# Batch 3's mixing behind steps with a product, partly on GpSimd, and two context moves later

## The reference, cut to what matters

```python
# first layer, on x of 4 batches x 1024 rows x 128 columns
x = layernorm_g_b(layernorm(x))
last_x = x shifted down by one row
k, v, r = [(x * m + last_x * (1 - m)) @ W.T for m, W in ((mix_k, Wk), (mix_v, Wv), (mix_r, Wr))]
den[t] = den[t-1] * td + exp(k[t]);  num[t] = num[t-1] * td + exp(k[t]) * v[t]     # td = exp(time_decay)
x2 = x0 + (sigmoid(r) * num / (den + 1e-8)) @ Wo.T
# second layer, on layernorm(x2): six nodes, each an attention of 8 heads
for c in range(6):
    q = ew[c,0] * (nodes[c-1] @ We[eq] + be[eq])
    k, v likewise from up to five nodes back
    o = softmax(qh @ kh.T / 4) @ vh, heads joined, @ Wo[c]
    nodes[c] = act_w[c] * o + q
out = x2 + layernorm(nodes[5]) * g + b
```

## Time and profile before

| | |
|---|---|
| median of 3 runs | 2249.14 us (2245.19 to 2252.85) |
| the profiled execution's own time | 2245.28 us |
| span of the profile | 2243.5 us |
| TensorE busy | 2182.0 us, 97% |
| VectorE busy | 2064.3 us, 92% |
| ScalarE busy | 1796.7 us, 80% |
| GpSimd busy | 530.1 us, 24% |
| mean granted TensorE clock | 0.994 |

### The profile page before, as it was taken

How to read it: one execution, slowest core, us unless ns; L and a number is a source line. 1 busy time by engine, 2 the same in 40 slices (tenths; PEclk the granted TensorE clock), 3 DMA queues, 4 the chain that set the end, 5 groups by cost and what they waited for, 6 DMA issues and landing times.

```text
span 2243.5 us, 43662 instructions
## 1 busy us (share of the span) xinstructions
PE 2182.0 (97%) x16565; PEld 885.5 (39%) x16565; DVE 2064.3 (92%) x3252; ACT 1796.7 (80%) x3432; POOL 530.1 (24%) x667
## 2 busy tenths in 40 slices
PE   7999999999999999999999999999999999999997
PEld 3533333343333443443433433433433434434332
DVE  6999999999989999999999999999999999999895
ACT  4377887888778888888888888888888888788776
POOL 4431221312203113123023022022121121431213
PEclk9999999999999999999999999999999999999999
DMA  4230422414223134133232242242242242241301
GB/s 127 65 75 22 83 55 67 81 45 85 60 59 80 50 72 82 53 81 73 54 79 65 58 83 58 56 93 55 59 84 55 57 85 54 59 99 43 75 25 53
DMA packets 87536, 149.39 MB, mean 67 GB/s; under 512 B 35146, under 2 KB 49950, under 8 KB 87326
## 3 DMA queue, kind: packets, MB, share of 16 engines
q0 software_dynamic: 28224, 94.13, 20.0%
q1 hardware_dynamic: 59102, 52.46, 9.4%
HBM read 42.36 MB, written 14.91 MB: 26 GB/s over the span
## 4 chain that ended last, share of the span: by engine, by line
PE 76%; DVE 11%; SPq 7%; DMA 4%; issue 2%; ACT 1%; POOL 0%; POOLq 0%; DVEq 0%; ACTq 0%
PE context L660 28%; PE ring L615 26%; PE wide L639 8%; DVE max_neg L1279 4%; SPq L1593 4%; DVE max_neg L1276 3%; PE wide L550 2%; PE wide L530 2%; PE wide L522 2%; DMA q_aug<-rows_dram 2%; DMA rows_dram<-max_turn 2%; PE wide L555 2%; SPq L1590 1%; PE wide L541 1%; PE context L485 1%
## 5 line engine op out<-in xcount | busy, mean ns | idle before, releaser
L906 ACT ACTIVATE e_ring<-ring 128x512 f32<-128x512 f32 x3053 | 1603.7, 602 | 302.6 <-PE ring L615 300.5
L1276 DVE TENSOR_REDUCE max_neg<-wide 128x1 f32<-128x512 f32 x1800 | 1132.7, 682 | 87.6 <-PE wide L639 84.5
L639 PE MATMUL wide<-k_aug,q_aug 48*128 48x512 f32 x3072 | 1057.3, 440 | 14.0 <-DVE max_neg L1279 6.7
L615 PE MATMUL ring<-q_aug,k_aug 50*128 50x512 f32 x3053 | 1042.6, 437 | 16.1 <-DMA q_aug<-rows_dram 15.2
L660 PE MATMUL context<-e_ring,v_aug 128*32 128x256 f32 (+1 forms) x9240 | 905.0, 463 | 1.0 <-ACT raw L915 0.9
L1279 DVE TENSOR_REDUCE max_neg<-wide 128x2 f32<-128x1024 f32 x636 | 771.8, 1218 | 26.3 <-PE wide L639 20.2
L615 PEld LDWEIGHTS ring<-q_aug,k_aug 50*128 50x128 f32 x3053 | 492.7, 185 | 726.0 <-ACT e_ring L906 608.5
L639 PEld LDWEIGHTS wide<-k_aug,q_aug 48*128 48x128 f32 x3072 | 500.2, 185 | 40.2 <-DVE max_neg L1279 15.8
L660 PEld LDWEIGHTS context<-e_ring,v_aug 128*32 128x32 f32 x9240 | 184.7, 108 | 412.1 <-issue 293.3
L395 POOL DMA_DIRECT2D src<-node_dram x40 | 22.9, 572 | 672.8 <-DMA rows_dram<-max_turn 672.8
L1381 POOL CAST q_part<-q_part 128x512 fp32r<-128x512 f32 x46 | 28.1, 611 | 397.5 <-DVE max_turn L1298 214.2
(11 more groups left out here) (245 smaller groups left out, 938.7 us busy)
## 6 DMA issues: line engine op xcount, KB each, us to landing
q_aug<-q_part POOLq DMA_DIRECT2D x138, 256.0 KB, 4.3
k_aug<-k_part POOLq DMA_DIRECT2D x138, 256.0 KB, 6.5
src<-node_dram POOLq DMA_DIRECT2D x40, 512.0 KB, 7.2
ctxT<-raw SPq DMA_DIRECT2D x380, 32.0 KB, 2.0
rden_bc<-rden_dram SPq DMA_DIRECT2D x23, 512.0 KB
node_dram<-node_ring SPq DMA_DIRECT2D x16, 512.0 KB, 2.7
q_aug<-rows_dram SPq DMA_DIRECT2D x192, 8.0 KB
node_ring<-in_L_attn_x SPq DMA_DIRECT2D x4, 512.0 KB, 5.3
```

Of the source, the lines that this page charges most:

```text
L615: e.matmul(bk[:, :], k_aug[first:first + AUG, u % 2, h // 2, chunk * P:(chunk + 1) * P].bitcast(F32R), q_aug[first:first + AUG, u % 2, h / ...
L639: e.matmul(bk[:, :], q_aug[first:first + SPLIT, u % 2, head // 2, q0:q0 + P].bitcast(F32R), k_aug[first:first + SPLIT, u % 2, head // 2, h ...
L906: e.activation(e_ring[:, n % E_SLOTS, :], bank[where["st", n]][:, :], ACT.Exp, scale=EXP_SCALE).then_inc(a_exp, 1)
L1276: e.tensor_reduce(max_neg[:, G % 2, kh, row:row + 1], wide[:, b, :], AX_X, ALU.max, negate=True).then_inc(v_mx, 1)
```

## The change

It has five parts.

1. **Row mixing on GpSimd.** For i = 6 and 7 the subtraction and the three blends leave VectorE (4 instructions a half) for GpSimd (7 a half: the subtraction, then a multiplication and an addition for each blend).
2. **Denominator product on GpSimd.** PRODUCT for i = 4 to 7 leaves VectorE (1 instruction a half) for GpSimd (2 a half). i = 4 and 5 are in unit 0 and start their product one step earlier.
3. **Batch 3's steps.** All of batch 3's stages now stand at the end of whole steps, and TensorE's stages of it on odd ones. Its TensorE products go to wide banks, behind the attention's product of that step and before the half weighted sum (`late_mix_at`). The table that predicts wide banks counts them.
4. **Two context moves.** The moves of a unit's first two groups, at steps 15 and 17 before, both stand at step 21, behind the rows' store of step 20 and their load. In the last unit this holds for the first group only.
5. **The last outputs.** Of unit 22's output projection, made in unit 23, the first half moves from step 13 to step 15.

A semaphore `v_num` takes the place of an engine-wide count for the numerator scan.

```diff
...
@@ -223,11 +223,13 @@
         LERPED = (6, 7)
+        ON_RING = (TURN, PROJ_K, PROJ_V, PROJ_R, OUT, TURN2)
+        GPSIMD_PRODUCT = (4, 5, 6, 7)
         COLUMNS_AT = 2
         EDGE_TURNS = -(-3 * NODES // 4)
 
         K_AT, OUT_AT, TURN_AT, V_AT, Q_AT = (7, 11), (15, 19), 21, (23, 27), (31, UC + 3)
-        FIRST_K_AT, FIRST_V_AT, FIRST_Q_AT, LAST_OUT_AT, LAST_TURN_AT = (5, 9), (21, 25), (2, 3), (13, 17), 19
+        FIRST_K_AT, FIRST_V_AT, FIRST_Q_AT, LAST_OUT_AT, LAST_TURN_AT = (5, 9), (21, 25), (2, 3), (15, 17), 19
...
-            (U1 + 4.5, U1 + 12.5, U1 + 13, U1 + 18, U1 + 29.5, U2 + 4.5, U2 + 6, U2 + 12.5, U2 + 6, U2 + 10, U2 + 14, U2 + 14,
-             U2 + 16.5, U2 + 29.5, U3 + 4.5, U3 + 12.5, U3 + 12.5, U3 + 16.5, U3 + 19, U3 + 22, U3 + 29.5, U4 + 4.5, U4 + 6, U4 + 10),
...
+            (U1 + 15, U1 + 31, U2 + 1, U2 + 5, U2 + 16, U2 + 16, U2 + 16, U2 + 16, U2 + 21, U2 + 25, U2 + 29, U2 + 29, U2 + 31, U3,
+             U3 + 15, U3 + 15, U3 + 31, U3 + 31, U4, U4 + 5, U4 + 15, U4 + 17, U4 + 18, U4 + 21),
...
-        LATE_R1_AT = {U2 + 22: 6, U5 + 22: 7}
+        LATE_R1_AT = {U2 + 30: 6, U5 + 15: 7}
...
-                taken += len(products(s))
+                taken += len(products(s)) + sum(k in ON_RING for _, k in mix_stages(s))
...
-                        e.wait_ge(v_lerp, 4 * LERPED.index(i) + n + 2)
+                        e.wait_ge(g_lerp, 3 * LERPED.index(i) + n + 1)
...
                 for i, k in mix_stages(s):
                     mix(i, k, next_bank)
 
+            def late_mix_at(s):
+
+                for i, k in mix_stages(s):
+                    mix(i, k, next_max_bank)
...
                 pair(s, 3)
                 pair(s + 1, 0)
                 weighted(s - 1, whole, True, True)
-                mix_at(s)
                 pair(s + 1, 1)
                 pair(s + 1, 2)
                 pair(s + 1, 3)
                 for kind, unit, hf in products(s + 1):
                     product(kind, unit, hf, next_max_bank())
+                late_mix_at(s + 1)
                 weighted(s, first_half, True, False)
-                mix_at(s + 1)
 
             alone[0] = True
             for s in range(ALONE, LAST_STEP):
...
-                if k == LERP_D and i in LERPED:
-                    e.wait_ge(a_xT, i + 1)
-                    e.tensor_tensor(y, xT[:, 1:BANK + 1], xT[:, 0:BANK], ALU.subtract).then_inc(v_lerp, 1)
-                if LERP_K <= k <= LERP_R and i in LERPED:
-                    n = k - LERP_K
-                    e.wait_ge(v_lerp, 4 * LERPED.index(i) + 1)
-                    e.scalar_tensor_tensor(out=(ek, ekv, er)[n], in0=y, scalar=col[:, C_MIX + n:C_MIX + n + 1], in1=xT[:, 0:BANK],
-                                           op0=ALU.mult, op1=ALU.add).then_inc(v_lerp, 1)
...
+                    if i in LERPED:
+                        e.wait_ge(g_lerp, 3 * LERPED.index(i) + 3)
...
-                if k == PRODUCT:
+                if k == PRODUCT and i not in GPSIMD_PRODUCT:
...
+                xT = mixing_xTs[i]
+                if k == LERP_D and i in LERPED:
+                    e.wait_ge(a_xT, i + 1)
+                    e.wait_ge(v_pad, i + 1)
+                    e.wait_ge(p_mt, i + 1)
+                    after()
+                    step(e.tensor_tensor(y, xT[:, 1:BANK + 1], xT[:, 0:BANK], ALU.subtract))
+                if LERP_K <= k <= LERP_R and i in LERPED:
+                    n = k - LERP_K
+                    dst = (ek, ekv, er)[n]
+                    after()
+                    step(e.tensor_scalar(dst, y, col[:, C_MIX + n:C_MIX + n + 1], None, ALU.mult))
+                    after()
+                    signal(e.tensor_tensor(dst, dst, xT[:, 0:BANK], ALU.add), g_lerp)
+                if k == PRODUCT and i in GPSIMD_PRODUCT:
+                    e.wait_ge(v_den, i + 1)
+                    e.wait_ge(v_ekv, i + 1)
+                    after()
+                    step(e.tensor_scalar(ek, y, WKV_EPS, None, ALU.add))
+                    after()
+                    signal(e.tensor_tensor(er, er, ek, ALU.mult), g_prod)
...
-                    if s % NCH == 1 and 0 <= G < GROUPS and G % GPU and G != GROUPS - 3:
+                    if s % NCH == 1 and 0 <= G < GROUPS and G % GPU > 1:
                         move_ctx(G)
                     if s == ALONE + 2:
                         move_ctx(GROUPS - 3)
-                    G = (s - 15) // NCH
-                    if s % NCH == 7 and 0 <= G < GROUPS and G % GPU == 0:
+                    G = (s - 21) // NCH
+                    if s % NCH == 5 and 0 <= G < GROUPS and G % GPU == 0:
                         move_ctx(G)
+                        if G + 1 != GROUPS - 3:
+                            move_ctx(G + 1)
```

More of the change, by code:

```diff
@@ L153, in build @@
         a_exp, a_k1, a_q1, a_oa, a_cv, a_ft, a_high, a_order = sems("a_exp a_k1 a_q1 a_oa a_cv a_ft a_high a_order")
-        v_own, v_omm, v_lerp, v_split0, v_var, v_y, v_pad, v_ekv, v_den, v_prod, v_inv, v_gate, v_x2, v_var2, v_n2 = sems(
-            "v_own v_omm v_lerp v_split0 v_var v_y v_pad v_ekv v_den v_prod v_inv v_gate v_x2 v_var2 v_n2")
+        v_own, v_omm, v_num, v_split0, v_var, v_y, v_pad, v_ekv, v_den, v_prod, v_inv, v_gate, v_x2, v_var2, v_n2 = sems(
+            "v_own v_omm v_num v_split0 v_var v_y v_pad v_ekv v_den v_prod v_inv v_gate v_x2 v_var2 v_n2")
         v_mx, v_cmb, v_neg, v_v, v_rec, v_fvar, v_ctx, v_lvar, v_z = sems(
             "v_mx v_cmb v_neg v_v v_rec v_fvar v_ctx v_lvar v_z")
-        g_own, g_half, g_ident, g_vones, g_kones, g_rs1, g_rs2, g_rsf, g_rsl, g_r1, g_gate = sems(
-            "g_own g_half g_ident g_vones g_kones g_rs1 g_rs2 g_rsf g_rsl g_r1 g_gate")
+        g_own, g_half, g_ident, g_vones, g_kones, g_rs1, g_rs2, g_rsf, g_rsl, g_r1, g_gate, g_lerp, g_prod = sems(
+            "g_own g_half g_ident g_vones g_kones g_rs1 g_rs2 g_rsf g_rsl g_r1 g_gate g_lerp g_prod")
         g_k, g_q, g_norm, g_out, g_y, g_n2, g_fn = sems("g_k g_q g_norm g_out g_y g_n2 g_fn")
@@ L253, in build @@
                              (-12, -12, -11, -10, -9, -9, -7, -6, -5, -5, -1)),
[2 rows of a table removed]
[L256 to L261 removed]
[2 rows of a table added]
+            (U1 + 15, U1 + 31, U2 + 1, U2 + 5, U2 + 16, U2 + 16, U2 + 16, U2 + 16, U2 + 21, U2 + 25, U2 + 29, U2 + 29, U2 + 31, U3,
+             U3 + 15, U3 + 15, U3 + 31, U3 + 31, U4, U4 + 5, U4 + 15, U4 + 17, U4 + 18, U4 + 21),
+            (U2 + 5, U2 + 21, U4 + 23, U4 + 29, U5, U5, U5, U5, U5 + 5, U5 + 9, U5 + 13, U5 + 13, U5 + 15, U5 + 16,
+             U5 + 31, U5 + 31, U6 + 1, U6 + 7, U6 + 9, U6 + 13, U6 + 15, U6 + 17, U6 + 18, U6 + 21))
+        LATE_R1_AT = {U2 + 30: 6, U5 + 15: 7}
         VALUES_FREE_AT = 18
@@ L1074, in mix @@
                     done = e.tensor_tensor_scan(num, td, ekv, 0.0 if hf == 0 else keep[1], ALU.mult, ALU.add)
-                    step(done)
+                    done.then_inc(v_num, 1)
                     if hf == 0:
-                        after()
+                        e.wait_ge(v_num, i + 1)
                         step(e.tensor_copy(keep[1], num[:, BANK - 1:BANK]))
-                if k == PRODUCT:
+                if k == PRODUCT and i not in GPSIMD_PRODUCT:
                     if i < EARLY:
@@ L1087, in mix @@
                     n = k - INV_A
-                    e.wait_ge(v_prod, i + 1)
+                    if i in GPSIMD_PRODUCT:
+                        e.wait_ge(g_prod, GPSIMD_PRODUCT.index(i) + 1)
+                    else:
+                        e.wait_ge(v_prod, i + 1)
                     e.reciprocal(ek[:, n * P:(n + 1) * P], er[:, n * P:(n + 1) * P]).then_inc(v_inv, 1)
```

2 lines of the change are left out of this document (removed), and 4 rows, old and new, of the table MIX_AT.

## The result

The changed kernel took 2208.78 us (median of 4 runs, 2203.92 to 2214.87) against 2249.14: a ratio of 0.983, 95% interval 0.981 to 0.986. That is 40 us less where 33 were forecast, inside the range. The profiled execution took 2205.83 (span 2204.0) against 2245.28 (span 2243.5).

What follows compares the result with a forecast made beforehand. The prediction took TensorE's row of matmuls, interrupted by VectorE and a late transfer, to bound the kernel. Its terms -15 + 3.5 - 19 - 1 = -31.5 gave 2213.8 to 2217.6 us; it said 2216, range 2203 to 2233.

Steps and rivals of the forecast that it cites:

- The late rows: Step 24 of all units: TensorE's wait for rows goes once the context moves stand behind the load; -15 us, bounds 0 and -18.
- The moves' new place costs nothing in a normal unit: Third group's context copy: transfers land at 824.5, ScalarE starts its copy at 830.62, so 6 us are left; cost nothing.
- The rival of 2273: First group's context lands too late, stopping ScalarE at step 24 of every unit; 2273 us at 8 us late; chance 4%.
- The last unit: Eight first-group transfers stand ahead of the second group's denominators, so ScalarE's wait ends later; +3.5 us, bounds 0 and +5.
- Batch 3: Units 1 to 6: instructions leave VectorE and mixing stands behind products; -23 us, bounds -31 and -5, -19 after 4 for meetings.
- 10.9 + 27.3 + 4.4 = 42.6: Units 1 to 6: TensorE's mixing, VectorE's mixing and two held instructions, added without overlap, make up the 42.3 us lost.
- VectorE's uncovered work: Batch 3's VectorE stages not hidden in gaps at their new steps: 4.3 us for i = 6, 3.9 for i = 7, together 8.2.
- the two meetings charged at 4: Unit 5: GpSimd's normalisation and its row mixing might each meet VectorE's two-input work; about even odds each, 4 us for both.
- The price of a meeting: GpSimd's two-input instruction holds VectorE's, stopping TensorE and lowering its clock; about 3 to 4 us per meeting.
- One input holds nothing: GpSimd's one-input instructions do not hold VectorE's two-input ones; by the opposing documented rule the sum is about 2 us worse.
- Only the instructions go: Rival for batch 3: VectorE's work costs its length anywhere, so only -7.4 us there; 2227 us; chance 19%.
- Parts 2 and 5: Unit 0's two products leave VectorE: -1 us, bounds -1.5 and +3; later last output half: 0, bounds -2 and +2.

Runs made afterwards that it cites:

- moves_alone: The kernel before with only the context moves changed (a unit's first two behind step 21); 2229.79 us, ratio to before 0.993.
- no_moves: The changed kernel with the context moves back at steps 9 and 15; 2225.62 us, ratio to before 0.990.
- the early move: The changed kernel with the last unit's first context move back behind step 15; 2204.43 us, ratio to before 0.981.
- places_alone: The changed kernel with batch 3's row mixing and all denominator products back on VectorE, new steps and banks kept; 2223.91 us, ratio to before 0.991.
- gpsimd_alone: The kernel before with row mixing and denominator products moved to GpSimd at the old steps, banks and moves; 2244.22 us, ratio to before 0.999.
- meet_one: The changed kernel with 20 added one-input GpSimd instructions, released when VectorE begins its maxima hand-over in units 8 to 17; 2213.78 us, ratio to before 0.985.
- best: The changed kernel with the last unit's first context move behind step 15 and two GpSimd instructions held until VectorE's hand-over; 2197.76 us, ratio to before 0.978.
- meet_late: The changed kernel with 20 added one-input GpSimd instructions, released one VectorE maximum before the hand-over; 2210.44 us, ratio to before 0.983.

## Why the prediction was right, step by step

- **The late rows (-15).** Right in mechanism and place, and near in size. Units 7 to 22 give 14.0 and units 1 to 6 another 2.0 (moves_alone) to 4.7 (no_moves): 16 to 19, about the upper bound of 18. In units 7 to 22 the 12.0 us of waits and the 1.7 of clock behind one of them are nearly all of the 14.0.
- **The moves' new place costs nothing in a normal unit.** Right: clean units are at 84.8 and ScalarE shows no wait there. The rival of 2273 fell.
- **The last unit (+3.5).** Right: 4.4, by the two steps that the early move takes back. It shows as only +1.2 in the last unit's total, since the kernel before had a meeting there at 2170, with TensorE stopped for 2.3 us and 3.4 us at half clock behind it, that the changed one's profile happened to miss:

```profile
2170.03 2.21 DVE L1285 TENSOR_TENSOR max_all<-max_neg 128x16 f32<-128x16 f32 x1
```

- **Batch 3 (-23, charged down to -19).** That VectorE's work costs less behind a product holds, the size was low: 23.7 (no_moves against before) to 26.4 (changed against moves_alone).
  - *The loss before.* Of the gain 5.1 and 6.8 are half clock that went with the two old meetings; 18.6 and 19.6 are left. The prediction had no such term: its 10.9 + 27.3 + 4.4 = 42.6 met the lost 42.3 by luck. With 5.1 us of clock in the 42.3, 37.2 are left for those three terms, so about 5 us of VectorE's work already overlapped in the kernel before, and "do not overlap at all" was too strong.
  - *The first mis-sized term of the sum* is VectorE's uncovered work: 8.2 forecast, 17 - 10.9 = 6 measured, 0.9 of that the doubled query product in unit 1 that both kernels have. Steps 31 of units 3 and 5, where I had two reciprocals at 1.3 us each, lose 0.1 and 0.0, though a reciprocal still takes 0.93. I had put each stage against the gap of its own step. My explanation, which fits these rows but was not tested by itself: banks are free ahead of VectorE, so what one step lacks the next ones give back, as long as TensorE does not run out of banks (places_alone, at 353.64).
  - *The second* is the two meetings charged at 4. Neither came, and both by little: in unit 5 the normalisation started 0.26 us behind the end of the hand-over's last two-input instruction (0.2 to 0.4 us in all eleven profiles with the new places), and the row mixing was met only late in a one-input instruction, its last two-input one starting 0.46 us behind the hand-over. Nothing in the prediction had worked out these small distances, so that part of the gain is luck:

```profile
593.00 0.17 DVE L1294 TENSOR_TENSOR max_part<-max_all,max_part 128x16 fp32r<-128x16 f32 x1
...
593.43 2.39 POOL L1438 TENSOR_TENSOR ctxT<-ctxT,rden_bc 128x1024 f32<-128x1024 f32 x1 [7.09 <-DMA rden_bc<-rden_dram]
```

```profile
569.39 1.57 POOL L1373 TENSOR_SCALAR mixing<-mixing,col 128x512 f32<-128x512 f32 x1
...
570.10 0.17 DVE L1289 TENSOR_TENSOR max_all<-max_neg 128x16 f32<-128x16 f32 x1
570.20 0.17 DVE L1290 TENSOR_TENSOR max_part<-max_neg 128x16 fp32r<-128x16 f32 x1
570.40 0.18 DVE L1294 TENSOR_TENSOR max_part<-max_all,max_part 128x16 fp32r<-128x16 f32 x1
...
571.04 1.29 POOL L1375 TENSOR_TENSOR mixing<-mixing,mixing_xT 128x512 f32<-128x512 f32 x1
```

- **The price of a meeting (3 to 4 us).** Wrong as a general price. It was read from a 2.4 us hold; a hold of 0.87 us costs 0.4. What makes it dear is a stop of TensorE with the half clock behind it: the two old meetings cost a stop of 1.4 to 1.5 us each and 3.4 to 10.2 us at half clock in the profiles of before, moves_alone and gpsimd_alone, together 3 to 7 us a piece.
- **One input holds nothing.** Wrong. The earlier trace rows showed VectorE 1.49 us behind the start of a group of three one-input instructions, and from that I took that they never hold; `meet_one` shows 0.45 us. The three took 2.59 us, 0.86 each, so by that estimate VectorE started some 0.6 us into the second, late enough to pass. The Trainium skill ("SBUF — State Buffer", Who interferes with whom) names any GpSimd instruction that reads SBUF. The runs agree with it on whether VectorE is held, and add that the hold of a one-input instruction ends long before the instruction does. The sum was not hurt.
- **"Only the instructions go".** As a theory of batch 3 it fell: the new places alone give 15.3 us, and at the old steps the instructions gave 2.9 (4.6 clear of the clock) where it says 7.4.
- **Parts 2 and 5 (-1, 0).** Part 2 is lost in unit 0's scatter (108.1 to 108.7) and no run tests it alone. Part 5: 0.

Not settled: the lead (100.7 to 102.2, and 106.4 in `best` and `meet_late`, where the clock stood at half speed for 10.2 us from 86.6) moves from run to run, and no experiment was aimed at it. Nor is it settled how the 15.3 us divide between the new steps and the new banks.

## What to carry to other kernels

- Where two engines keep pace, ask first where work stands and only then how much there is. 15 us came from the new places (steps with a product, and wide banks), 3 at most from taking instructions off VectorE at the old steps, and 11 more from GpSimd once the new places had put those stages together.
- A move of transfers on an in-order queue is worked out from issue times (0.62 us each here), separately for the last unit, where a group has more of them and nothing follows to hide them.
- Small meetings of GpSimd and VectorE that depend on when a transfer lands make a kernel scatter. Two more waits on the engine with slack kept TensorE's stop in unit 0 at 0.8 us instead of 1.85, with no half clock behind it; the median was 6.6 us lower, in runs that overlap.
- Compare stages of two kernels with the half-speed time taken out. It differed by 3.4 us between profiles of units 1 to 6 with the same two stops, as much as some of the effects measured here.
